# Two experts for each token instead of all eight: rows sorted through main memory into 40 tiles of 128 places

## The reference, cut to what matters

```python
scores = softmax((x @ wt.T + repeat(g @ wg.T, 64)) / 2)     # 8 experts
topk_w, topk_idx = top_k(scores, 2)                          # two for each token
topk_w = topk_w / (topk_w.sum(-1) + 1e-20)
gp = leaky(einsum('th,ehm->etm', x, w_gate))                 # e = 8, h = 256, m = 128
up = einsum('th,ehm->etm', x, w_up)
y_all = einsum('etm,emh->eth', gp * up, w_down)
y = (y_all[topk_idx, arange(T)] * topk_w).sum(1)
p = leaky(x @ sw_gate) * (x @ sw_up) @ sw_down               # shared, width 256
moe = y + p
out = x + relu(moe @ W1 + b1) @ W2 + b2                      # 256 -> 1024 -> 256
```

## Time and profile before

| | us |
|---|---|
| median of 3 runs | 616.28 (615.48 to 617.25) |
| the profiled execution | 616.01 |
| its span, first to last instruction | 614.3 |
| PE busy | 563.7 (92%) |
| DVE busy | 423.0 (69%) |
| POOL busy | 317.3 (52%) |
| ACT busy | 230.1 (37%) |
| mean granted TensorE clock | 0.987 of full speed |

### The profile page before, as it was taken

One profiled execution on the slowest core, in us unless ns is written; L12 is line 12 of the kernel. 1 busy time (PEld: TensorE's weight loads), 2 busy tenths in 40 slices (PEclk: granted clock), 3 DMA queues, 4 the chain that ended last, 5 costly groups with the idle time before them and its releaser, 6 DMA issues.

```text
span 614.3 us, 10676 instructions
## 1 busy us (share of the span) xinstructions
PE 563.7 (92%) x3499; PEld 472.4 (77%) x3499; DVE 423.0 (69%) x966; ACT 230.1 (37%) x469; POOL 317.3 (52%) x280
## 2 busy tenths in 40 slices
PE   1178799999999999999889999999999999999997
PEld 0166689999999999998766778877798777977776
DVE  3598889999999999988566667464465645555432
ACT  1344355555555555554213332222322222222221
POOL 4077678787878787875133224432244232433243
PEclk9998899999999999999989999999999999999999
DMA  5581000000000000000031000100001000010001
GB/s 159 157 147 36 27 2 27 2 26 0 26 0 27 0 26 0 26 1 28 0 124 39 2 0 1 35 2 0 1 1 36 0 0 0 0 34 1 0 1 34
DMA packets 29167, 15.76 MB, mean 26 GB/s; under 512 B 13968, under 2 KB 28624, under 8 KB 29136
## 3 DMA queue, kind: packets, MB, share of 16 engines
q1 hardware_dynamic: 29136, 15.36, 9.3%
HBM read 13.00 MB, written 2.36 MB: 25 GB/s over the span
## 4 chain that ended last, share of the span: by engine, by line
PE 47%; DVE 5%; ACT 1%; issue 1%; DVEq 0%; POOL 0%; ACTq 0%; POOLq 0%
PE bank L239 8%; PE bank L240 7%; PE bank L241 7%; PE bank L1258 7%; PE bank L1261 3%; PE bank L244 3%; PE bank L245 3%; PE bank L1312 2%; PE bank L1267 2%; DVE lk L973 1%; PE bank L1298 1%; DVE hw L982 1%; PE bank L1220 1%; DVE wk L934 1%; ACT gs L634 0%
## 5 line engine op out<-in xcount | busy, mean ns | idle before, releaser
L491 POOL TENSOR_TENSOR hl<-hw,hh 128x512 fp32r<-128x512 f32 x40 | 51.6, 1291 | 123.4 <-ACT hh L256 123.4
L973 DVE SCALAR_TENSOR_TENSOR lk<-gs 128x512 f32<-128x512 f32 x40 | 44.1, 1103 | 57.5 <-ACT gs L634 57.5
L494 POOL TENSOR_TENSOR hl<-hw,hh 128x512 fp32r<-128x512 f32 x32 | 41.2, 1287 | 59.0 <-ACT hh L651 58.6
L256 ACT ACTIVATE hh<-hw 128x512 fp32r<-128x512 f32 x40 | 25.3, 632 | 106.2 <-DVE hw L987 47.2
L239 PE MATMUL bank<-x1T_h,wu_h 128*128 128x512 f32 x160 | 63.3, 396 | 0.5 <-DVE xs L864 0.5
L241 PE MATMUL bank<-x1T_h,wu_l 128*128 128x512 f32 x160 | 63.0, 394 | 0.0
L240 PE MATMUL bank<-x1T_l,wu_h 128*128 128x512 f32 x160 | 62.9, 393 | 0.0
L477 POOL TENSOR_TENSOR rn<-sc,half 128x5 f32<-128x5 f32 (+1 forms) x32 | 54.8, 1729 | 1.8 <-DVE sc L839 1.7
L1008 DVE TENSOR_SCALAR hw<-bank,b1c 128x512 f32<-128x512 f32 x32 | 24.0, 751 | 30.3 <-PE bank L241 25.5
L651 ACT ACTIVATE hh<-hw 128x512 fp32r<-128x512 f32 x32 | 20.2, 632 | 63.5 <-PE bank L1312 43.9
L470 POOL TENSOR_TENSOR sim<-sim,mx 128x1040 f32<-128x1040 f32 x16 | 30.9, 1932 | 19.3 <-DVE mx L824 19.0
(11 more groups left out here) (248 smaller groups left out, 1597.3 us busy)
## 6 DMA issues: line engine op xcount, KB each, us to landing
fstage<-in_f_W SPq DMA_DIRECT2D x4, 512.0 KB, 5.0
out<-obuf SPq DMA_DIRECT2D x8, 256.0 KB, 2.2
xs<-in_x SPq DMA_DIRECT2D x1, 1536.0 KB, 9.3
raw_qkv<-in_c_Wq SPq DMA_DIRECT2D x1, 1024.0 KB, 5.9
raw_out<-in_c_Wout SPq DMA_DIRECT2D x1, 1024.0 KB, 8.3
stage<-in_m_wgate SPq DMA_DIRECT2D x8, 128.0 KB, 2.2
stage<-in_m_wup SPq DMA_DIRECT2D x8, 128.0 KB, 2.3
stage<-in_m_wdown SPq DMA_DIRECT2D x8, 128.0 KB, 2.3
```

Source lines behind the costliest of these rows:

```text
L491: e.tensor_tensor(hl[:, u % 2, :], hw[:, u % 2, :], hh[:, u % 2, :].bitcast(F32), ALU.subtract).then_inc(sems['hl'], 1)
L494: e.tensor_tensor(hl[:, j % 2, :], hw[:, j % 2, :], hh[:, j % 2, :].bitcast(F32), ALU.subtract).then_inc(sems['fl'], 1)
L973: e.scalar_tensor_tensor(lk[:, :], gs[:, :], 0.01, gs[:, :], ALU.mult, ALU.max).then_inc(sems['lk'], 1)
```

## The change: what it does

Shared units and the dense network keep their shapes. The routed experts are done another way.

- **Router.** The tokens are transposed four times as before (`x_transpose`, into `x1A` and `x1B`, kept for all 2048 tokens). The logits now have tokens on the partitions: for each of 16 tiles, six products with 8 columns, and one of 32 columns a group for the part of `g`. DVE works in three batches, of 8, 4 and 4 tiles (`router_logits`, `router_top`, `router_places`). It marks the two experts of each token (`oh`), and a product with a triangle of ones (`ranks`) says how many tokens before this one chose the same expert: the token's place in that expert's list (`posi`). `slot_table` computes on DVE, from the eight counts, which expert and which rows each of 40 tiles takes (`tab_u`, `tab_row`), and where a token finds its results (`yrow`).
- **Scatter.** `xdram` in main memory has 17408 rows of 1 KB; during attention SP fills it with zeros in four parts of 4.46 MB. POOL writes each token's row to its two places: 32 indirect DMAs of 128 rows.
- **Slots.** 20 pairs of tiles of 128 places. SP reads a row number from `tab_row` into a register and loads 128 rows; PE transposes them, reads the expert's number from `tab_u` (a TENSOR_LOAD, twice for gate and up and twice for down in each pair), and multiplies by that expert's weights with a register in the address. The results are stored to `ydram`.
- **Gather.** POOL fetches each token's two result rows by indirect DMA (32 of 128 rows), and DVE weights and adds them to the shared expert's output (`mix`), which is transposed for the dense network. Group 0's eight gathers wait for all stores; those of group g+1 stand between the `hl` of the dense network in group g.
- Shared units 0 to 5 run between the attention and the slots, 6 and 7 after them; their `hl` moves from POOL to DVE.

```diff
+BATCHES = ((0, 8), (8, 4), (12, 4))
+SLOTS = 2 * T // P + E
+PAIRS2 = SLOTS // 2
+ROWS = E * CAP + E * P
+XQ = 4
...
# SyncE
+            with e.Fori(0, ZPARTS) as x:
+                e.wait_ge(sems['unit'], due(x + NS))
+                load_unit(gate_e, up_e, down_e, bass.ds(x, 1))
+                e.dma_start(zero_v[bass.ds(x, 1), :, :, :].rearrange('c p q d -> p (c q) d'), zrow[:, :].rearrange('p (o d) -> p o d', o=1).to_broadcast([P, ROWS // P // ZPARTS, D])).then_inc(sems['st_zero'], 16)
...
+            def load_slots(s):
+                if s >= XQ:
+                    e.wait_ge(sems['bx_t'], due(s - XQ + 1))
+                for t in range(2):
+                    row_j = e.value_load(tab_row[0:1, 2 * s + t:2 * s + t + 1], min_val=0, max_val=ROWS - P)
+                    e.dma_start(xq[:, s % XQ, t, :], xdram.ap()[bass.ds(row_j, P), :]).then_inc(sems[f'ld_xq{s % XQ}'], 16)
...
+            e.wait_ge(sems['tab'], 3)
+            e.wait_ge(sems['st_x'], 16 * 2 * NT)
...
# GpSimd
+            for b, (t0, n) in enumerate(BATCHES):
+                e.wait_ge(sems['pos'], due(b + 1))
+                for t in range(t0, t0 + n):
+                    for r in range(2):
+                        e.indirect_dma_start(out=xdram.ap()[:, :], out_offset=bass.IndirectOffsetOnAxis(ap=posi[:, t, r:r + 1], axis=0), in_=xs[:, t, :], in_offset=None).then_inc(sems['st_x'], 16)
...
+            for c in range(2):
+                e.wait_ge(sems[f'st_y{c}'], 16 * (PAIRS2 // 2))
+            for t in range(TG):
+                gather(0, t)
+            for g in range(G):
+                for j in range(FB):
+                    e.wait_ge(sems['fh'], due(FB * g + j + 1))
+                    e.tensor_tensor(hl[:, j % 2, :], hw[:, j % 2, :], hh[:, j % 2, :].bitcast(F32), ALU.subtract).then_inc(sems['fl'], 1)
+                    if g + 1 < G and j < TG:
+                        gather(g + 1, j)
...
# VectorE
+            def after_step_before_last():
+                x_lower(2)
+                router_logits(0)
+                router_top(0)
...
+            def mix(g):
+                e.wait_ge(sems[f'ld_g{g % 2}'], 16 * 2 * TG * (g // 2 + 1))
...
+                for t in range(TG):
+                    i = g * TG + t
+                    last = e.scalar_tensor_tensor(yg[:, g % 2, 0, t, :], yg[:, g % 2, 1, t, :], topw[:, i, 1:2], yg[:, g % 2, 0, t, :], ALU.mult, ALU.add)
+                last.then_inc(sems['yv'], 1)
...
# TensorE
+            def slot_gate_up(s):
+                e.wait_ge(sems['bxl'], due(s + 1))
+                e.wait_ge(sems['bh'], due(s - 1))
+                for t in range(2):
+                    u = e.value_load(tab_u[0:1, 2 * s + t:2 * s + t + 1], min_val=NS, max_val=U - 1)
+                    dst = bank[2 + s % 2][:, t * D:(t + 1) * D]
+                    for k in range(KD):
+                        last = split_passes(e, dst, (bxT_h[:, s % 2, t, k, :], bxT_l[:, s % 2, t, k, :]), (slot_weights(wu_h, u, k), slot_weights(wu_l, u, k)), k == 0, k == KD - 1)
+                last.then_inc(sems['bgu_t'], 1)
...
+            for s in range(PAIRS2):
+                if s + 1 < PAIRS2:
+                    slot_transpose(s + 1)
+                slot_gate_up(s)
+                if s >= 1:
+                    slot_h_transpose(s - 1)
+                if s >= 2:
+                    slot_down_project(s - 2)
```

More of the change, by code:

```diff
@@ L624, in _ @@
[L624 to L644 removed]
+                e.activation(dst, fstage[:, c % 2, :], ACT.Copy).then_inc(sems['f_h'], 1)
@@ new lines, in shared_out @@
+            def shared_out(g):
+                e.wait_ge(sems['down_t'], due(NS * (g + 1)))
+                for c in range(2):
+                    e.activation(p_all[:, g * TG + 2 * c:g * TG + 2 * c + 2, :], bank[2 + c][:, :].rearrange('p (t n) -> p t n', t=2), ACT.Copy).then_inc(sems['p'], 1)
+            x_upper(3)
+            router_exp(1)
+            unit(0)
+            router_exp(2)
+            unit(1)
+            unit(2)
+            unit(3)
+            shared_out(0)
+            unit(4)
@@ new lines, in first_x, with first_logits, second_logits @@
+            def first_x():
+                e.wait_ge(sems['sim'], due(NB3 * NT))
+                e.wait_ge(sems['ld_late'], 16 * (KD + 4))
+                for t in range(NT):
+                    last = e.matmul(bank[1][0:2, t * E:(t + 1) * E], condT[:, 2 * t:2 * t + 2], wgT[:, 0:E], start=True, stop=True)
+                last.then_inc(sems['lg_t'], 1)
+                x_transpose(0)
+            def first_logits():
+                logits(0)
+                x_transpose(1)
+            def second_logits():
+                logits(1)
+                x_transpose(2)
@@ new lines, in _ @@
+            pipeline(e, body, {-1: after_first_projection, 0: after_first_scores, 1: after_second_scores, NT + 1: second_logits})
+            e.wait_ge(sems['x1'], due(NT))
+            e.wait_ge(sems['unit'], NS)
+            ranks(0)
+            x_transpose(3)
+            gate(0)
+            e.wait_ge(sems['pos'], 1)
+            logits(3)
+            gate(1)
+            up(1)
+            ranks(1)
+            gate(2)
+            up(2)
+            down(0)
+            ranks(2)
+            counts()
@@ new lines, in _ @@
+            e.wait_ge(sems['tab'], 2)
+            e.wait_ge(sems['pos'], due(NB))
+            e.wait_ge(sems['hw'], EARLY)
+            e.wait_ge(sems['p'], 2 * (EARLY // NS))
+            e.wait_ge(sems['unit'], U)
+            slot_transpose(0)
+            for s in range(PAIRS2):
+                if s + 1 < PAIRS2:
+                    slot_transpose(s + 1)
+                slot_gate_up(s)
+                if s >= 1:
+                    slot_h_transpose(s - 1)
+                if s >= 2:
+                    slot_down_project(s - 2)
@@ new lines, in _, with y_transpose @@
+            e.wait_ge(sems['bxl'], due(PAIRS2))
+            gate(6)
+            slot_h_transpose(PAIRS2 - 1)
+            slot_down_project(PAIRS2 - 2)
+            up(6)
+            slot_down_project(PAIRS2 - 1)
+            gate(7)
+            up(7)
+            down(6)
+            down(7)
+            def y_transpose(g):
+                e.wait_ge(sems['yv'], due(g + 1))
+                e.wait_ge(sems['yT_l'], due(KD * g))
+                for k in range(KD):
+                    for t in range(TG):
+                        last = e.transpose(bank[k][:, t * P:(t + 1) * P], yg[:, g % 2, 0, t, k * P:(k + 1) * P], ident[:, :])
+                    last.then_inc(sems['yT_t'], 1)
@@ L1317, in group @@
+                    last = e.matmul(place[t], hl[:, j % 2, t * P:(t + 1) * P], w2_h[:, j, :], start=False, stop=j == FB - 1, skip_group_check=True)
+                    if j == FB - 1 and t == 1:
+                        last.then_inc(sems['f2_c'], 1)
+                last.then_inc(sems['f2_c' if j == FB - 1 else 'f2_t'], 1)
+            for g in range(G):
                 for j in range(FB + 2):
                     if j < FB:
-                        first(j)
-                    if j == 1 and more:
-                        logits_transpose(g + 1)
```

981 lines of the change are left out of this document (557 added, 424 removed).

## The result

The changed kernel took 618.15 us (median of 11 runs, 616.43 to 619.18), the kernel before on the same chip 616.28 (11 runs). The ratio is 1.0029, 95% interval 1.0015 to 1.0042: no gain, a loss of 0.3%. The forecast was 588 us. Two later groups of runs, each on a chip of its own, make the loss 2.9% and 0.6%; the second half of this document is about the difference. The profiled execution took 617.8 us and has a span of 616.0; the one before took 616.0 and had a span of 614.3.

A forecast was written before the change was run, and what follows sets the result against it. PE was taken to bound the kernel, busy 92% of the span. 616.0 - 153.3 - 13.6 + 15.4 + 18.2 + 83 + 16.3 + 6.6 = 588.6 us, 8-in-10 range 552 to 636.

The forecast's parts named there:

- What goes: In the groups, 32 routed units leave, 153.3 us, and the router's work on PE, 13.6 us.
- the zeros: Zero fill of main memory during attention: a 4.46 MB part lasts 23 us, units come 31 us apart, so hidden.
- the gather: From the last slot's product at 461.5 to the dense network at 481.7 us; 16.3 us of it new.
- Tail of attention: Attention's last steps: more PE work, a 6 us wait for `at`, 1.2 us for the clock; ends 15.4 us later.
- To the first slot: Between attention and slots, POOL's 32 indirect DMAs at 1.1 us put the first slot at 374; costs 18.2 us.
- Slots: PE's instruction stream, not its array, sets a pair at 4.1 us; 20 pairs take 83 us.
- L: Cost of one TENSOR_LOAD on PE in the slots, four a pair: 0.5 to 0.56 us, less 0.2 a pair.
- Dense network: Transposes 2.6 us, POOL's gathers and `mix` 4 us in all for three groups: 6.6 us more.
- Table reads: Rival: the slots' 80 TENSOR_LOADs stall PE, at 1.1 us each a pair takes 6.7 us, time 640; chance 0.11.
- POOL at 1.65: Rival: POOL bounds scatter, gather and dense groups, 631 us at 2 us an indirect DMA, deciding from 1.65; chance 0.10.
- The slow clock in the slots: Rival: gaps drop PE to 1.2 GHz in the slots, a pair takes 5.3 us, time 617; chance 0.05.

The follow-up runs named there:

- at_first_up: Changed kernel with DVE doing `at` ahead of the router's first batch in attention's last step, PE's `up(0)` behind the last value products; 625.34 us, ratio 1.016.
- reads_fixed: Changed kernel with PE taking each slot's expert as a constant, its 80 table reads left out (some slots use wrong weights); 587.14 us, ratio 0.9525.
- reads_ahead: Changed kernel with PE reading a pair's two experts once, a pair ahead behind 12 products, 40 reads instead of 80; 597.49 us, ratio 0.9706.
- no_gather: Changed kernel without the 24 gathers of groups 1 to 3; 602.51 us, ratio 0.9768.
- scatter16: Changed kernel with 16 of the 32 scatter DMAs, only the rows of each token's first expert; 612.39 us, ratio 0.9941.
- reads_packed: Changed kernel with eight slots' experts packed in one number by DVE, PE reading five numbers ahead of the slots; 607.58 us, ratio 0.9873.
- best: Changed kernel with packed experts read before the last early down product, `at` before router, `hl` on DVE, paced gathers, four early units; 562.63 us, ratio 0.9136.
- groups B and C: Two sets of runs, each on one chip: four edits of the changed kernel (607.58 to 633.97 us); then its repeat and three variants (587.36 to 635.11 us).
- late_no_scatter: Changed kernel with `gate(6)` and `up(6)` behind the last slots' products and without the 32 scatter DMAs; 615.76 us, ratio 1.0004.
- after_again: The changed kernel itself, unchanged, run once more on another chip; 632.94 us, ratio 1.0291 to the kernel before.
- late_again: Repeat of the changed kernel with `gate(6)` and `up(6)` moved behind the last slots' products; 635.11 us, ratio 1.0326.
- hl_dve: Changed kernel with the dense network's `hl` made by DVE one step behind `hw`, instead of by POOL; 632.44 us, ratio 1.027.

## Why the prediction was wrong, by its own steps

The end came 29.1 us later than forecast: 3.2 by the last `xs`, 7.8 more by the first slot, 9.1 in the slots, 0.7 to the dense network and 8.3 in it. Two steps failed by their mechanism, the slots and the dense network; two terms were too small.

- **What goes, the zeros, the gather.** 153.3 + 13.6 us less and zeros at no cost were taken over, and nothing contradicts them: attention up to 265 us runs as before, and the parts of zeros land in 14.4 us within the 31 us between units. From the last slot's product to the dense network it is 20.9 us for 20.2.
- **Tail of attention (+15.4): mechanism right, 3.2 us short.** The wait of 6 us for `at` came with 5.9; the low clock costs some 3.4 us, not 1.2. at_first_up removes the wait, and the last `xs` comes 8.4 us earlier.
- **To the first slot: right that POOL sets it, 7.8 us more.** The 32 indirect DMAs take 41.3 us and not 32 x 1.1 = 35.2, 6.1 us more; the start, counted from the last `xs`, is 1.2 us later, and the rest is landing.
- **Slots: this step failed by its mechanism.** L was nearly right (0.42 us measured, 0.45 taken), but I set the pair at the stream's 2.3 + 4 L and let the array's 2.8 run beside it. The two add up instead: a pair is the array's 2.9 plus 4 L, 4.6, and reads_fixed shows both terms. That is 9.1 us in all. Why they add up is argued and not shown: PE stands at a semaphore ahead of each group, so it has few products queued when a read comes. reads_ahead bears it out in part, a read behind 12 products costs 0.30 us and not 0.42.
- **Dense network (+6.6): this step failed too.** I gave POOL 3.5 us in each of four steps and wrote that it "catches up in the other four". A late step isn't made good when PE has no slack, and `mix`, put behind step 5, waits on DVE for the last landing (3.27 us in the row at 551.57). no_gather prices the gathers at 15.6 us for my 4; the rest of this stretch was 3.3 us cheaper than I had counted, so 8.3 us show at the end.
- **The rivals.** Table reads would have had to cost 0.85 us: no. POOL at 1.65: no, it is 1.26, though its two places (first slot, dense steps) are where 18 us of the difference lie (6.1 and 11.6). The slow clock in the slots: no, 0.50 lasts until 392.4 and from there to 484.4 it is 1.00. None of the rivals alone was the case; four terms, each 3 to 12 us too small, were, less the 3.3 us by which the rest of the dense network was counted too dear. The Trainium skill, SBUF — State Buffer, section Who interferes with whom, has descriptors held up while DVE runs an operation that takes the shared port pair. This trace shows only little of it for the scatter (a DMA of 1.21 or 1.29 us beside DVE's `hl` instead of 0.96, some 1 us in all), while for elementwise work on POOL beside DVE the delay is plain (`hl` 2.85 us in scatter16).
- **What no term of the sum had**: on two of the five groups' chips the other engines' streams are held up beside the scatter, DVE's above all, and the change costs 2.9%. The forecast's own runs don't have this; it is no part of the 29.1 us.

## What to carry to other kernels

Price a table read on an engine's stream at the work that it empties, on top of the array's time and not beside it. Eight small numbers packed in one read took 29 us back here (first slot to last store 67.9 us in reads_packed, 97.2 in the changed kernel). An engine that paces a loop can't catch up in the loop's other half if the engine it feeds has no slack: spread its work evenly, one DMA a step. And before a chain is shortened, look at what stands behind it on its engine, since that moves forward too and may meet a neighbour. When the same program is slower on another chip, look for the engine on the chain that ended last before the one whose gaps catch the eye.

## What the runs showed of the hardware

- A scatter or gather of 128 rows of 1 KB takes POOL 0.96 us and 1.26 us from one to the next; it lands 2.4 us (scatter) or 2.7 us (gather) behind its start. Beside DVE's `hl` some took 1.1 to 1.3 us in the changed kernel's trace, and 1.41 and 1.47 in best.
- A table read on PE takes 0.30 us, 0.68 with its checks and address; in the slots 0.42 us of PE's time, 0.30 behind 12 products. The Trainium skill, DMA: Bandwidth & Descriptors, section Latency and other measured facts, gives the read itself about 0.6; the measurement decides.
- While POOL's indirect DMAs go out in a row, PE may issue one instruction in 0.7 us or a multiple, and DVE none for up to 20 us, until 2.5 to 4 us behind the last one queued; PE's stretch begins 15 to 18 us behind the first. Of the scatter's bursts on these chips those of 16 and 24 had it, those of 8 did not. All seven traces with the scatter in groups B and C showed it, on two chips, and none of the nine elsewhere, the changed kernel's own first trace among them; late_no_scatter, on one of the two chips, did not. It cost 15 us in one and the same program. The Trainium skill, Runtime: NRT & Kernel Launch, section Instruction fetch mechanics, holds that fetching instructions is hidden behind the pace of issue. The traces give no sign that these gaps are fetches: of the queues that the view of DMAs calls `instruction`, one moved a single piece (16 KB, 1.38 us) between 352 and 371 in after_again, as in the changed kernel's own trace, and none moved anything there in late_again and hl_dve.
